# Attention of layer 1: the diagonal of batches 6 and 7 is masked on VectorE by a minimum with a table

## What is computed

```python
attn = jnp.einsum('bnih,bjh->bnij', q, k)
causal = jnp.triu(jnp.ones((S, S), dtype=bool), 1)
attn = jnp.where(causal, -jnp.finfo(attn.dtype).max, attn)
attn = jax.nn.softmax(attn, axis=-1)
out = jnp.einsum('bnij,bjd->bind', attn, v)
out = out.reshape(B, S, N_HEADS * HEAD_DIM)
out = out @ w_proj.T + b_proj
```

## Time and profile before

| | |
|---|---|
| median of 3 runs | 1161.76 us (1159.61 to 1175.99) |
| the profiled execution | 1172.08 us, span 1169.5 us |
| PE busy | 899.2 us (77%) |
| DVE busy | 685.6 us (59%) |
| POOL busy | 621.2 us (53%) |
| ACT busy | 467.1 us (40%) |
| L1414 on POOL, both layers | 107.5 us in 256 operations |
| L1553 on POOL | 125.2 us in 128 scatters |
| mean granted clock of TensorE | 0.851 |

### The profile page before, as it was taken

The page is one execution under the profiler, slowest core; times in us unless marked ns, Lnnn a source line. Parts: engine busy times, 40 slices in busy tenths (PEclk is TensorE's granted clock), DMA queues, the critical chain, the costliest instruction groups (busy, mean ns, idle before and its releaser), DMA issues.

```text
span 1169.5 us, 22075 instructions
## 1 busy us (share of the span) xinstructions
PE 899.2 (77%) x5927; PEld 691.8 (59%) x5927; DVE 685.6 (59%) x2692; ACT 467.1 (40%) x1176; POOL 621.2 (53%) x870
## 2 busy tenths in 40 slices
PE   1687989878597992379987888856899999989900
PEld 1465667657355881256665565533688887778700
DVE  4678888865532554467687674352455544444568
ACT  2346666743112441257655443311344444444400
POOL 3646666523163652336558888755356655545500
PEclk9859999988798996559989576787999999999955
DMA  8500000000624543400002222566455655545287
GB/s 231 192 2 1 2 2 1 1 2 1 263 106 127 152 130 120 144 1 2 2 29 86 85 97 101 210 222 221 147 163 174 182 157 161 153 141 156 70 327 319
DMA packets 73093, 136.97 MB, mean 117 GB/s; under 512 B 13406, under 2 KB 51725, under 8 KB 70928
## 3 DMA queue, kind: packets, MB, share of 16 engines
q1 hardware_dynamic: 52144, 85.15, 22.8%
q0 software_dynamic: 17632, 46.73, 11.2%
q10 hardware_dynamic: 3200, 3.70, 0.9%
HBM read 79.15 MB, written 62.39 MB: 121 GB/s over the span
## 4 chain that ended last, share of the span: by engine, by line
PE 36%; DVE 9%; POOL 6%; issue 5%; ACT 2%; another core or an unknown queue 1%; DMA 1%; DVEq 0%; POOLq 0%; ACTq 0%; SPq 0%
PE s_psum L1996 12%; PE s_psum L2009 6%; PE s_psum L1988 3%; POOL rows L1553 3%; PE s_psum L1477 3%; PE s_psum L2004 2%; DVE a_masked L1074 2%; DVE f_rows L2096 2%; DVE f_xT L2096 2%; PE s_psum L549 1%; POOL a_probs L1414 1%; PE s_psum L1496 1%; PE s_psum L646 1%; PE s_psum L602 1%
## 5 line engine op out<-in xcount | busy, mean ns | idle before, releaser
L2106 POOL DMA_INDIRECT parts<-e_y,e_dest x206 | 202.7, 984 | 180.7 <-DVE e_y L2079 96.9
L1996 PE MATMUL s_psum<-wres,e_xT 128*128 x824 | 213.9, 382 | 1.8 <-ACT e_xT L2036 1.0
L1996 PEld LDWEIGHTS s_psum<-wres,e_xT 128*128 128x128 f32 x824 | 156.1, 191 | 26.1 <-issue 5.4
L1414 POOL TENSOR_SCALAR_AFFINE_SELECT a_probs<-a_probs 128x256 f32<-128x256 f32 x256 | 107.5, 444 | 117.6 <-ACT a_probs L870 116.8
L1553 POOL DMA_INDIRECT rows<-f_rows,f_place_at x128 | 125.2, 978 | 40.3 <-issue 31.7
L2009 PE MATMUL s_psum<-wres,e_hT 128*128 x412 | 125.3, 386 | 12.2 <-ACT e_hT L2046 11.6
L870 ACT ACTIVATE a_probs<-s_psum 128x768 f32<-128x768 f32 x128 | 104.6, 817 | 72.8 <-PE s_psum L629 68.2
L2041 ACT ACTIVATE e_act_out<-s_psum 128x128 f32<-128x128 f32 x206 | 57.1, 277 | 180.8 <-PE s_psum L1996 101.6
L2070 DVE TENSOR_TENSOR e_hid<-e_act_out,s_psum 128x128 f32<-128x128 f32 x206 | 59.0, 286 | 91.8 <-issue 42.6
L1074 DVE CUSTOM_DVE_ANT_0 a_masked<-s_psum,a_ahead 128x128 f32<-128x128 f32 (+1 forms) x256 | 76.1, 353 | 42.0 <-PE s_psum L605 39.1
L2079 DVE TENSOR_SCALAR e_y<-s_psum,e_xg 128x256 f32<-128x256 f32 x206 | 99.6, 484 | 0.7 <-issue 0.7
(11 more groups left out here) (297 smaller groups left out, 1993.4 us busy)
## 6 DMA issues: line engine op xcount, KB each, us to landing
e_xg<-rows SPq DMA_DIRECT2D x159, 160.0 KB
f_rows<-parts SPq DMA_DIRECT2D x8, 1024.0 KB, 7.2
f_xT<-parts SPq DMA_DIRECT2D x8, 1024.0 KB, 7.4
wres<-in_experts SPq DMA_DIRECT2D x21, 384.0 KB
e_xg<-rows SPq DMA_DIRECT2D x47, 144.0 KB
wres<-in_experts SPq DMA_DIRECT2D x4, 1536.0 KB
rows<-empty SPq DMA_DIRECT2D x1, 5120.0 KB, 24.1
e_yk<-parts SPq DMA_DIRECT2D x16, 256.0 KB, 2.9
```

What stands on the lines that cost most here:

```text
L1414: last = nc.gpsimd.affine_select(out=diagonal[:, :, a], in_=diagonal[:, :, a], compare_op=ALU.is_ge, fill=0.0, base=0, pattern=[[0, 2], [1 ...
L1996: last = nc.tensor.matmul(ps_u[b % 2][:, 0:2 * P], xT[b % 2][:, c * P:(c + 1) * P], wres[:, ds(e, 1), 2 * c * P:2 * (c + 1) * P].rearrange ...
L2106: nc.gpsimd.indirect_dma_start(out=parts[:, :], out_offset=bass.IndirectOffsetOnAxis(ap=dest[b % NY][:], axis=0), in_=y[b % NY][:], in_off ...
```

## The change

Of layer 1's eight batches, batches 6 and 7 are now masked on DVE. DVE makes a table once, `causal`, which holds 3.0e38 where the query is at or behind the key and 0 elsewhere, and takes the minimum of the two diagonal blocks and the table, in one operation for each pair of heads. PE waits for a semaphore of its own for these batches. DVE masks a pair one slot later in the lists than POOL did: behind the maxima of the next slot, and the eighth pair in slot 0 of the next round. Layer 0 and batches 0 to 5 of layer 1 stay as they were.

```diff
+    first_dve_cut = B if front is None else B - 2
+            causal = sb("causal", [P, P])
             def attend(s, i):
-                pe.wait_ge(cut_done, PAIRS * s + 2 * i + 2)
+                if s < first_dve_cut:
+                    pe.wait_ge(cut_done, PAIRS * s + 2 * i + 2)
+                else:
+                    pe.wait_ge(dve_cut, PAIRS * (s - first_dve_cut) + 2 * i + 2)
+            def cut(s, j):
+                dve.wait_ge(exp_done, PAIRS * s + j + 1)
+                diagonal = probs[:, j % NPB].rearrange("p h (a k) -> p h a k", k=P)[:, :, 0:3:2]
+                nc.vector.tensor_tensor(diagonal, diagonal, causal[:].unsqueeze(1).unsqueeze(1).to_broadcast([P, 2, 2, P]),
+                                        ALU.min).then_inc(dve_cut, 1)
+
                 dve_route.start(0)
+                step(nc.vector.tensor_tensor(causal[:], tri_r[:].bitcast(F32), ident[:], ALU.add))
+                step(nc.vector.tensor_scalar(causal[:], causal[:], BIG, None, ALU.mult))
                     if live(i):
                         maxima(i, j)
+                    if j and live(i - 1) and i - 1 >= first_dve_cut:
+                        cut(i - 1, j - 1)
+                    if j == 0 and live(i - 2) and i - 2 >= first_dve_cut:
+                        cut(i - 2, PAIRS - 1)
-                    if live(i - 1):
+                    if live(i - 1) and i - 1 < first_dve_cut:
                         cut(i - 1, j)
```

## The result

The changed kernel takes 1185.26 us (median of 4 runs, 1182.92 to 1188.86), the kernel before in the same comparison 1167.96 us (median of 4, 1159.61 to 1175.99). The ratio is 1.0187, with a 95% interval of 1.0142 to 1.0233. The ratios in this text compare undisturbed executions alone and are estimates with an interval, not the quotient of the two medians, which here is 1.0148. So the loss is 17.3 us by the medians and 21.8 us by the ratio. The forecast was 1158.0 us and a range that ended at 1168.

What follows compares the result with a forecast made beforehand. PE's waits for POOL's masks and the clock drop behind them were taken as the bound in rounds 7 and 8, not POOL itself; +1.4, -0.2 and -5.0 sum to -3.8 us, from the median 1161.76 to 1158.0 us, range 1150 to 1168.

Steps and rivals of the forecast that it cites:

- Setup: Making the table with two small DVE operations ahead of the rounds: hidden, cost 0; under 1.4 us if the cover were gone.
- price of a minimum: One minimum on DVE: 0.69 us, ends 0.66 and 0.90; 16 of them 11.0 us of DVE's time.
- PE's waits for masks: PE's two waits for POOL's masks in rounds 7 and 8 go: -1.6 us, 1.4 of it at slot (8, 5).
- POOL: Rounds 7 and 8: 10.4 us of POOL's time freed, only 1.6 us on the path; round 9's scatters at most 3.0 us earlier.
- the stalls in round 11 move: Rival, round 11: ACT's 12.29 us and DVE's 9.86 us unexplained waits change by -6 to +6 us; chance 0.12.
- No mechanism here reaches it: Whole kernel: no listed mechanism reaches a 2% change, 23 us; the largest are 10.4 us down and 9.4 us up.
- The clock: End of round 8: without PE's 1.39 us wait TensorE holds 2.4 GHz, so L716 starts 5.0 us earlier; chance 0.37.
- PE's waits for DVE at the end of round 7: End of round 7: two minima ahead of the maxima and chosen experts add 1.4 us, about 3.0 instead of 1.6.
- POOL was the bound after all: Rival, rounds 7 and 8: all 10.4 us of POOL's time comes back, giving 1151.4 us; chance 0.06.
- Its waits for DVE behind round 8: Behind round 8 POOL waits 8.35 us for batch 7's statistics and 4.58 us for its places, so POOL isn't the bound there.
- The points named as proof of error: Wrong if PE waits over 1 us for `dve_cut`, rounds 7 to 9 lengthen, or the last part shifts more than rounds 7 and 8.

Runs made afterwards that it cites:

- e10: The kernel before with batches 6 and 7 masked by nobody, neither selects on GpSimd nor minima on DVE; 0.9919 on a chip of the first kind.
- e8: The changed kernel, unedited, run again on a chip of the first kind (before 1138.85 us); 0.9935.
- e6: The changed kernel, unedited, run again on a chip of the second kind (before 1173.9 us); 1.0244.
- e5: The kernel before, unchanged, run again on a chip of the second kind (before 1173.9 us); 1.0002.
- e11: The kernel before plus two idle selects on GpSimd in each slot of rounds 9 to 11, on a chip of the first kind; 1.0165.
- e2: The changed kernel plus two idle selects on GpSimd in each of the 16 old mask places, on a chip of the first kind; 1.0032.

## Why the prediction was wrong

**Setup, price of a minimum, PE's waits for masks: right.** 0.69 us each (682 to 693 ns), taken as 0.69. The upper end of 0.90, which I had set beside a rule of the Trainium skill (GPSIMD Engine Reference, Key points: contention with VectorE instructions that have two SBUF inputs), wasn't reached: all 16 minima, most of them beside scatters, lie within 11 ns of each other. No contention with scatters shows. The kernel without minima (e10, 0.9919) and the one with them (e8, 0.9935) differ by less than their intervals. By these ratios the 16 cost some 2 us of their 11.0 on the path (0.0016 x 1139), by rounds 7 and 8 of the two profiles 3.3 us (48.7 against 45.4).

**The step that failed is "POOL".** It read "On the path only the two waits go" and "POOL's scatters of round 9 can start at most 3.0 us earlier". I took GpSimd's freed time as idle time at worst. But its next work is a queue of DMAs that nothing else holds back. With the masks gone the sixteen scatters of round 7 start within 19.7 us instead of 23.8, and on this kind of chip round 7 becomes 10.5 us longer and round 8 4.5 (13.8 and 8.6 in e6 against e5). In rounds 7 and 8 the prediction put this effect at nothing. A hint stood in my own rows. The earlier trace rows hold starts late with ready inputs in a stretch of unbroken scatters, and I filed them under "the stalls in round 11 move", with "either sign alike" and a size of 6 us. I never asked why no such stall stands in rounds 4 to 8, where a pair of scatters goes out each 3.19 us. That question leads to a better rival: more rounds of the kind that already stalls, each with the excess of such a round.

**"No mechanism here reaches it", said of 2%, was argued from the wrong list.** "The largest are 10.4 us down and 9.4 us up" counted only the work that the change moves, not what the moved work triggers. From the trace of before, round 11 holds 5.7 us of late start on ACT and about 6.5 us on DVE, one behind the other, so an estimate of one stalled round is 12 us and of two 24 us. That alone would have put a loss of 2% within reach. The measured lengths are 10.5 and 4.5 us for rounds 7 and 8, so the size would still have been too high, and it goes by a single round.

**The clock: right.** In e8 the router's matmuls of round 8 run at the fast level:

```profile
700.11 1.08 PE L713 MATMUL s_psum<-router,f_xT 128*128 128x32 f32 x8
708.58 0.45 PE L616 MATMUL s_psum<-ident_r,a_max_stack 128*128 128x128 f32 x3 [1.69 <-DVE a_max_stack L1092]
710.74 0.29 PE L722 MATMUL s_psum<-ident_r,a_chosen_r 128*32 128x128 f32 x2 [0.46 <-DVE a_chosen_r L1183]
723.91 1.08 PE L713 MATMUL s_psum<-router,f_xT 128*128 128x32 f32 x8
732.48 0.29 PE L722 MATMUL s_psum<-ident_r,a_chosen_r 128*32 128x128 f32 x2 [2.24 <-DVE a_chosen_r L1183]
```

1.08 us in both rounds, where round 8 of before had 1.92. On the same chip e11, whose round 8 has the masks on POOL as before, waits 0.80 us for a mask and then has 1.92 us too, so the gain isn't the chip's:

```profile
719.02 1.08 PE L648 MATMUL s_psum<-a_probs,a_v 128*32 128x256 f32 x8 [0.80 <-POOL a_probs L1416]
720.46 1.92 PE L709 MATMUL s_psum<-router,f_xT 128*128 128x32 f32 x8
```

PE's waits for DVE at the end of round 7 of e8 are 1.69 + 0.46 = 2.15 us (forecast 3.0), at the end of round 8 2.24 (forecast 1.4). In the profile of the result L713 takes 1.08 us in round 8 too (at 730.15 us), as forecast. There the hold-ups take the clock back in round 7: L713 has 1.92 us (at 695.31), where before had 1.08, and the clock is 0.50 in 700 to 710 us, the level of 1.2 GHz, behind 10 us in which PE was busy for 5.29.

**"POOL was the bound after all" was closer than its 0.06.** On the first kind of chip the changed kernel is 7.4 us faster (0.0065 x 1138.85; interval 3.8 to 11.0), the forecast said 3.8. Rounds 7 and 8 of e8 are 1.8 and 4.2 us shorter than those of e11, where the forecast had 1.4 us longer and 5.2 shorter. e2 puts the selects back beside the minima and costs 11.0 us more than e8 (1.0032 against 0.9935, from two chips of this kind), about the 10.4 us of POOL's time. There POOL's work seems to stand on the path. Its waits for DVE behind round 8, my evidence against, don't belong to the kernel on every chip. They are absent in e8, where `front_rstd` of rounds 9 and 10 follows without a wait.

**The points named as proof of error** did their work: the time between rounds 7 and 9 grew, by 15.0 us (68.7 against 53.7). The other two didn't occur: no row shows PE waiting for a minimum for over 1 us, and the last part, from L722 of round 9 to the experts, is 6.9 us longer, less than rounds 7 and 8.

## What to carry to other kernels

Work on an engine that issues DMAs can also be a pace for these DMAs. Before taking it away, ask what the engine will issue sooner and how densely, and look in the same trace for a stretch that is already that dense: if other engines start late there with ready inputs, the change may make more of it. Price a stall without a named cause as a possible cost of what runs beside it, and take off the part in which an input wasn't there yet. And compare two versions on more than one chip before believing a per cent: here the sign of the change depends on the chip (0.9935 on one, 1.019 to 1.024 in three comparisons on others).

## What the runs showed of the hardware

- Two kinds of chips. The same kernel takes 1138 to 1139 us on the two chips of the first kind and 1161 to 1174 us on those of the second (medians). Round 7 of the same code differs by 15.5 us (25.5 and 41.0 us, e8 and e6), at the same scatter rate. The experts take 319 to 320 us in the profiles of the first kind and 327 to 347 us in those of the second.
- On the second kind the traces hold fewer events. The page's list of DMA issues gives the time from issue to landing for the gathers of rows on the first kind and can't give it on the second (e8, then the changed kernel of the result):

```profile
e_xg<-rows SPq DMA_DIRECT2D x159, 160.0 KB, 2.3
```
```profile
e_xg<-rows SPq DMA_DIRECT2D x159, 160.0 KB
```

  The trace of e8 has 15,523 semaphore events, that of the result's changed kernel 9,896; both have the same number of DMA packets (73,106 and 73,107). All 20 traces fall so: 15,500 to 15,571 events in the eight of the first kind, 9,679 to 10,659 in the twelve of the second. The Trainium skill (NOTIFIC — the notification-queue block, Overflow: three behaviours, one of which stalls the engine) says that the block which writes such records pushes back inside rather than losing one, and that this could slow an engine. By that rule the late starts would fit and the missing records would not, and no run here tests it. Each execution in these comparisons comes with its span and granted clock, so none shows the times without such records. Whether the writing of records holds the engines up, or the signals of the DMAs are late, stays open. The fetch of instructions is unlikely: between 690 and 715 us, where e6's long round begins, the DMA queues (packets, MB, share) show two fetches beside the 854 packets of the scatters.

```profile
q0 software_dynamic: 854, 2.90, 31.6%
q8 instruction: 1, 0.02, 0.3%
q14 instruction: 1, 0.01, 0.1%
```

  What is shown is that scatters in close succession bring it about in rounds 7 and 8, on one kind of chip, and that a limit of two under way in these rounds, which also slows them, takes it away.
- A GpSimd select that does nothing useful, two per slot, costs 5.4 us a round where scatters fill the engine (21.8 to 27.2 us, e8 and e11): there GpSimd's list sets the round.
